# Attention stage of a small vision tower: where the output products of the preceding head stand in TensorE's order

## The reference, cut to what matters

```python
def _L1_attn_ref(x, Q, K, VO):
    d = x.shape[-1]                                  # 64
    q = jnp.einsum('btd,hrd->bhtr', x, Q)            # 8 heads, r = 32
    k = jnp.einsum('bud,hrd->bhur', x, K)
    scores = jnp.einsum('bhtr,bhur->bhtu', q, k) / sqrt(d)
    attn = jax.nn.softmax(scores, axis=-1)
    ctx = jnp.einsum('bhtu,bud->bhtd', attn, x)
    return jnp.einsum('bhtd,hde->bte', ctx, VO)
h = h + _L1_attn_ref(_layernorm(h, axis=-1), L1_attn_Q, L1_attn_K, L1_attn_VO)
```

## Time and profile before

| what | value |
|---|---|
| median of 3 runs | 629.54 us (629.16 to 629.71) |
| the profiled execution's own time | 629.09 us |
| its span, first to last instruction | 627.3 us |
| mean granted TensorE clock | 0.975 of full speed |
| PE (matmul) busy | 570.2 us, 91% of the span |
| DVE (VectorE) busy | 382.5 us, 61% |
| ACT (ScalarE) busy | 334.8 us, 53% |
| POOL (GpSimd) busy | 73.8 us, 12% |

### The profile page before, as it was taken

One profiled execution on the slowest core, in us unless ns is written; L12 is line 12 of the kernel. 1 busy time (PEld: TensorE's weight loads), 2 busy tenths in 40 slices (PEclk: granted clock), 3 DMA queues, 4 the chain that ended last, 5 costly groups with the idle time before them and its releaser, 6 DMA issues.

```text
span 627.3 us, 10237 instructions
## 1 busy us (share of the span) xinstructions
PE 570.2 (91%) x3082; PEld 339.8 (54%) x3082; DVE 382.5 (61%) x896; ACT 334.8 (53%) x735; POOL 73.8 (12%) x88
## 2 busy tenths in 40 slices
PE   0597797998899999999999999999999999997992
PEld 0353344653446657667666566665666766462441
DVE  3847458133587767767677577676776775135561
ACT  0455857765555646556466465564654655626411
POOL 0000000000499010010100101001001010102000
PEclk9999799999898999999999999999999999998997
DMA  7500000000363232332322323323233220000024
GB/s 166 221 0 2 0 0 2 0 1 1 84 149 81 72 86 70 83 87 56 99 69 73 94 56 87 81 62 99 63 79 89 57 74 1 1 1 1 1 51 103
DMA packets 21986, 37.65 MB, mean 60 GB/s; under 512 B 5560, under 2 KB 15224, under 8 KB 21704
## 3 DMA queue, kind: packets, MB, share of 16 engines
q1 hardware_dynamic: 21816, 37.12, 23.1%
q10 hardware_dynamic: 144, 0.20, 0.2%
HBM read 6.07 MB, written 2.41 MB: 14 GB/s over the span
## 4 chain that ended last, share of the span: by engine, by line
PE 86%; DVE 4%; ACT 4%; DMA 3%; issue 1%; SPq 1%; DVEq 0%; ACTq 0%
PE P L679 82%; DMA X<-x 2%; PE P L695 2%; ACT L481 1%; DVE xhat L1205 1%; PE P L941 1%; ACT PT L590 1%; ACT g L622 1%; DVE xs L1274 1%; PE P L1080 0%; PE P L814 0%; SPq L370 0%; DVE gate_s L1262 0%; DMA Ks<-QKH 0%; DVE bst L1142 0%
## 5 line engine op out<-in xcount | busy, mean ns | idle before, releaser
L1379 DVE TENSOR_REDUCE mx<-P 112x1 f32<-112x392 f32 x448 | 218.9, 558 | 96.6 <-PE P L679 92.3
L590 ACT ACTIVATE PT<-P 112x392 f32<-112x392 f32 x448 | 188.1, 494 | 26.3 <-PE P L679 25.3
L679 PE MATMUL P<-Ks,Qs 96*112 96x392 f32 x448 | 168.1, 380 | 0.8 <-DVE mx L1379 0.7
L679 PE MATMUL P<-Qs,Ks 98*112 98x392 f32 x448 | 155.0, 350 | 0.8 <-ACT PT L590 0.7
L679 PE MATMUL P<-PT,XVs 112*64 112x392 f32 x896 | 154.5, 496 | 0.0
L679 PEld LDWEIGHTS P<-PT,XVs 112*64 112x64 f32 x896 | 61.6, 137 | 79.4 <-issue 73.4
L679 PEld LDWEIGHTS P<-Ks,Qs 96*112 96x112 f32 x448 | 78.6, 177 | 43.0 <-issue 19.6
L598 ACT ACTIVATE CT<-P 128x392 f32<-128x392 f32 x32 | 15.9, 497 | 134.4 <-PE P L679 134.4
L679 PEld LDWEIGHTS P<-Qs,Ks 98*112 98x112 f32 x448 | 79.8, 179 | 6.1 <-ACT PT L590 3.7
L665 POOL TENSOR_TENSOR OUT<-OUT,part 120x448 f32<-120x448 f32 x27 | 30.7, 1136 | 274.2 <-DVE part L1406 274.2
L679 PE MATMUL P<-VBs,CT 128*112 128x130 f32 (+1 forms) x320 | 40.0, 261 | 0.6 <-ACT CT L598 0.6
(11 more groups left out here) (180 smaller groups left out, 513.9 us busy)
## 6 DMA issues: line engine op xcount, KB each, us to landing
Qs<-QKH SPq DMA_DIRECT2D x64, 98.0 KB, 2.2
Ks<-QKH SPq DMA_DIRECT2D x64, 98.0 KB, 2.2
XVs<-XV SPq DMA_DIRECT2D x32, 196.0 KB, 2.5
Qs<-QKL SPq DMA_DIRECT2D x32, 98.0 KB, 2.1
Ks<-QKL SPq DMA_DIRECT2D x32, 98.0 KB, 2.1
X<-x SPq DMA_DIRECT2D x4, 588.0 KB
out<-OT SPq DMA_DIRECT2D x24, 98.0 KB
wa<-table_a SPq DMA_DIRECT2D x1, 2207.5 KB, 8.3
```

Of the source, the lines that this page charges most:

```text
L590: nc.scalar.activation(PT[:, u, c * HALF:(c + 1) * HALF], P[0:T, SCORE_BANK + half_in_loop(s, u, c) % RING, 0:HALF], ACT.Exp, scale=float( ...
L679: return nc.tensor.matmul(dst, lhsT, rhs, start=start, stop=stop, **more)
L1379: nc.vector.tensor_reduce(mx[:, s % 2, c, t:t + 1], bank(n)[0:T, :], AX.X, ALU.max)\
```

## The change

The constant `OUT_AT` and the call of `head_out` at u = 3 and u = 5 go. Both halves of `head_out` are called one after the other behind the last pair of the score phase, ahead of the first context tile. No other engine's list is changed, nor any buffer, bank or semaphore count.

```diff
-        TURN_AT, OUT_AT = 1, (3, 5)
+        TURN_AT = 1
...
-                        if u in OUT_AT and not (first and s == 0):
-                            head_out(i if s else i - 1, (s - 1) % 4, first and s == 1, OUT_AT.index(u))
                         for c in range(2):
                             j = half_in_loop(s, u, c)
                             if more:
                                 max_half(*ahead, u, c, j % RING, last_in_bank(j))
                             score_half(i, s, u, c, first)
+                    if not (first and s == 0):
+                        for half in range(2):
+                            head_out(i if s else i - 1, (s - 1) % 4, first and s == 1, half)
                     for u in range(NT):
                         context_tile(i, s, u, first and s == 0)
```

## The result

The changed kernel takes **648.75 us** (median of 4 runs, 647.47 to 649.02) against 629.61 us for the kernel before beside it (629.16 to 629.71). The ratio is 1.0301, with a 95% interval of 1.0284 to 1.0319. The profiled execution took 649.02 us, with a span of 647.2 us and a mean granted clock of 0.969.

A forecast was written before the change was run, and what follows sets the result against it. TensorE carries the chain, but VectorE's 0.474 us step paces the score phase. 0.70 us more in each of 29 heads (20.3) plus 1.5 for heads 30 and 31 gives 21.8 on 629.54: 651.3 us, range 647 to 658.

The forecast's parts named there:

- VectorE sets the pace, 0.22 us come back: Score phase: VectorE's 0.474 us step sets the pace, so moving the products regains only the late eleventh maximum's 0.22 us.
- The 0.06 us that I took: Score phase: assumed delay from the eleventh maximum's end to the fourteenth matmul of the maxima, half the traced 0.12 us.
- TensorE's own pair: Score phase: TensorE needs 0.37 us per pair of maxima and score matmuls, against VectorE's 0.474 us.
- VectorE's rest ahead of a head: Before a head's first maximum: VectorE's rest, up to 3.0 us, was to grow by about 0.9 us.
- The block: Behind the last score: ten product records cost 0.97 us (0.94 to 1.00), plus 0.05 us of step before the context phase.
- the 0.10 us of step: Last score to first context matmul: 0.10 us beyond the usual 0.17; 0.05 was taken to remain behind the products.
- The context phase keeps 4.75 us: Context phase of each head: its length stays 4.75 us, with the next head starting right behind it.
- my 0.62 for the lower end: Heads 1 to 29: the lower end of the added time per head, 0.62 us, with 0.70 forecast and 0.78 the upper end.
- Heads 30 and 31: Last two heads, without maxima, paced by ScalarE: moved products cost 0.76 us each, 1.5 us for both.
- the one gap that I counted: Heads 30 and 31: tile 5's products hold ScalarE up by 0.21 us, which moving them gives back.
- The clock: Rival, context phases: short waits drop TensorE's clock to 1.2 GHz, adding 147 us, about 799 us; chance 0.02.
- VectorE's divide, GpSimd, SyncE: Other engines: later products make nobody wait; stack transfers start 1.8 us later with 2.1 us of slack left; cost nothing.

The follow-up runs named there:

- e5: Kernel before the change, with each row maximum taken over 280 of the 392 columns: 624.03 us, ratio 0.9941.
- e6: Changed kernel, with each row maximum taken over 280 of the 392 columns: 625.3 us, ratio 0.9934 to the kernel before.
- e10: Kernel before, products in four pieces: three at tiles 2, 3, 4, the last (two products of 65 columns) behind the last score: 625.33 us, ratio 0.9923.
- e2: Kernel before, with only half 1 of the products (6 records) moved behind the last score, half 0 left at tile 3: 629.84 us, ratio 1.0034.
- e1: Kernel before, with the products in four pieces at tiles 2, 3, 4 and 5 in place of two at 3 and 5: 623.82 us, ratio 0.9927.
- e4: Changed kernel with every output product done twice in the block behind the last score: 683.71 us, ratio 1.0865 to the kernel before.

## Why the prediction was right

Forecast 651.3 us, range 647 to 658, measured 648.75. By its own steps:

- **VectorE sets the pace, 0.22 us come back.** Right to the hundredth: last score at 6.09 us (6.10 forecast), the regained time 6.32 - 6.09 = 0.23, no late maximum, a beat of 0.47. The 0.06 us that I took, half-way, for the start behind the eleventh maximum is what the changed kernel shows (314.37 to 314.43). e5 and e6 show the pace as the cause and not only as a likeness. TensorE's own pair is 0.36 us and not 0.37, and VectorE's rest ahead of a head grew by 0.8 us and not 0.9.
- **The block.** Too dear: 0.97 + 0.05 forecast, 0.91 measured up to the first context matmul. The 1.00 us of the earlier trace rows held a start after a wait, and the 0.10 us of step, of which I kept half, are paid inside the block (0.21 us in place of 0.11, 315.43 to 315.64), where its full-width matmuls give way to half-width ones (e10).
- **The context phase keeps 4.75 us.** It became 4.71, as in e2, e6 and e10, where small products stand right in front of it; 4.75 or 4.76 in e1 and before, where they do not.
- So a head costs 0.54 to 0.55 us and not 0.70, below my 0.62 for the lower end: 16 us for 29 heads in place of 20.3. This is the mis-sized term, and the head is 11.90 us and not 12.04.
- **Heads 30 and 31.** Half the forecast price in the one undisturbed (0.38 against 0.76): the last score came 0.4 us earlier in the head (551.46 - 546.52 = 4.94 against 535.63 - 530.30 = 5.33), not the 0.21 of the one gap that I counted.
- **The clock.** I gave it 2 in 100 as a fall in every context phase. That did not happen: between 205 and 560 us the clock stayed at 1.00, although TensorE waited 249 times for VectorE. But one short fall did come, in head 31 from 562.7 us on, worth 1.6 us (12.45 - 10.84). The Trainium skill's "TensorE: Matmul & The Clock Gate", section "A second HAM failure mode: psum-queue depth-cycling", warns of just such frequent short idling. By these rows it came true in one of the two heads with scores alone (clock 0.86 over head 31), and not in the 29 with maxima as well (1.00).
- **VectorE's divide, GpSimd, SyncE** at nothing: right. The reciprocal starts 7.80 us into the head (8.03 before). SyncE's stack transfers start 8.85 us into it, 2.07 later than before, and the next on that queue 2.50 us into the next head.

That the total came so near is in part luck. I had 5.3 us too much for the heads (20.3 - 15.8 and twice 0.38), and had foreseen neither the 1.6 us of clock in head 31, nor the 1.3 us behind the attention, nor the 0.5 ahead of it. By what the heads alone cost (15.8 + 0.8 = 16.6 us on top of 629.54) the time would be 646.1 us, just under the range of 647 to 658. The mechanism was right, the price of the block too high.

## What to carry to other kernels

An engine that carries the whole chain of waits may still be paced by another one through the release of a few buffers: compare the steps of both engines, pair by pair, before pricing a move. Independent work on the paced engine is free only in pieces that fit its lead (0.36 us here with three banks), with enough pairs between them to regain it (four pairs did here, two left 0.08 us), and it is paid in full the moment it stands where nobody else is the brake. So spread it; four pieces in place of two gained 0.7%.

## What was not expected of the hardware

- Going from full-width matmuls to ones that write halves of the partitions costs about 0.10 us once (0.27 to 0.28 us from start to start in place of 0.17 to 0.18), and small half-width products right in front of the context phase shorten it by 0.04 us.
- The first two records of a product behind a score cost TensorE 0.14 us together (e10: 302.75 to 302.89), a further record 0.11 each, the four of 65 columns behind each other 0.16. But the next matmul then takes 0.26 to its follower (302.89 to 303.15) where 0.18 is usual, so such a piece costs 0.22 in all where nothing hides it. The same step, 0.27 for 0.18, stands behind each wait for VectorE (310.65 to 310.92 in the changed kernel).
- TensorE's clock held 1.00 through 29 heads with a wait of 0.2 us in 9 of 14 pairs, and fell to 0.50 in one of the two last heads (in e4 in both), whose scores wait about 0.2 us for ScalarE with no products between. With even one piece of products left among those scores (e2) it held. Why one head and not the other stays open; no run here tells it apart.
